# First attention of a two-layer transformer: the order of TensorE's work in a unit written out, and the row maxima split on GpSimd ahead of one transpose

## The chip, the cores and the metric

The kernel runs on one core of a Trainium2 chip. The metric is the device time of one execution in microseconds; before the change it is 1112.01 us, the median of three runs (1110.85 to 1116.76). Engines are named TensorE (PE), VectorE (DVE), ScalarE (ACT), GpSimd (POOL) and SyncE (SP), which issues the DMAs.

## The reference

The kernel computes two layers, each an attention and a mixture of experts. Only the first attention is touched by the change. With B = 2, S = 1024, D = 128, 16 heads of width 8:

```python
xn = _layernorm(x, ln_scale, ln_bias)
q = (xn @ wq).reshape(bs, sl, h, hd).transpose(0, 2, 1, 3)
k = (xn @ wk).reshape(bs, sl, h, hd).transpose(0, 2, 1, 3)
v = (xn @ wv).reshape(bs, sl, h, hd).transpose(0, 2, 1, 3)
scores = jnp.einsum('bhid,bhjd->bhij', q, k)
probs = jax.nn.softmax(scores / jnp.sqrt(jnp.float32(HIDDEN_DIM)), axis=-1)
out = jnp.einsum('bhij,bhjd->bhid', probs, v)
out = out.transpose(0, 2, 1, 3).reshape(bs, sl, -1) + xn
```

The softmax needs each query's maximum over 1024 keys, and it is exact: the maximum is subtracted before the exponential.

## The kernel before, in words

**Tiling.** Two heads make a pair, and 16 pairs (both batches) are worked on one after the other. A unit is one pair with one half of the queries (512), so there are 32 units (`UNITS0`); pair `u // 2`, half `u % 2`. Queries and keys are split in three bfloat16 parts each and stacked on 48 partitions (`q_stack`, `k_stack`), the two heads of a pair at partitions 0 and 64, so that a product of bfloat16 rows gives scores near float32. Two further rows of `q_stack` hold the negative maximum of each query as two bfloat16 parts (high and the rest); `k_stack` has ones there, so a score matmul of 50 rows subtracts the maximum.

**The two passes of a unit.** First the search: eight searches (`search`, L532 for TensorE and L396 for VectorE). Each is two matmuls of 128 queries by 512 keys (both heads) into a bank pair of the ring `max_bank`, and a VectorE maximum over it (L400). After the eighth, VectorE joins the halves (L406) into `maxima`, 128 queries x 8. TensorE transposes this to 8 x 128 (L548, "turn"), VectorE splits it in the bfloat16 parts with two instructions (L413, L415), and SyncE copies them with two DMAs into the two rows of `q_stack` (`subtract`, L275). Then the scores: 16 matmuls of 128 keys by 512 queries (`score`, L580) into three score banks, 16 exponentials on ScalarE (L509) into `probs` (four steps deep), and four value groups (`use`, L593) of four matmuls that add up in one bank. ScalarE copies that bank to `heads` (L481), TensorE turns it (`fold_heads`, L555), and VectorE divides by the sums (L423, L426).

**The ring and the order.** Searches, turns and folds share the ring of two (`RING = 2`). A use of the ring has a number, `PLACE`, the same on TensorE and VectorE, and TensorE may give place i only after VectorE has released place i-2 (`freed`). The order is written out by `ring_of_step`: in unit u at step k (0 to 7) the search number 8u + k + 12 is given (`LEAD = 12`), the turn of unit u+1 follows at step 4 and the fold of unit u-1 at step 6. TensorE's program (end of `layer0`) runs in each step: two scores, the ring's events, and after steps 1, 3, 5, 7 a value group (at step 1 the last one of the unit before). Every engine runs its instructions strictly in this program order. Ahead of unit 0 stand 12 searches and the turn of unit 0 (`ring_before`).

**Waits that matter here.** A score waits for the exponential three scores back (three banks). ScalarE waits before each even step for the value group that frees its `probs` buffer. The first score of a unit waits for the shift DMAs (`shift_in`). The first search of a pair waits for all of the pair's 12 stack loads (`loaded`, L538 with `loads_by`). Each head of a pair takes six loads.

**SyncE's queue.** Its loop over u issues `subtract(u + 1)`, which waits for the turn of unit u+1, and only then `load_head(u // 2 + 2, u % 2)`: the second head of pair p is issued behind the turn of unit 2p-2, which is given in unit 2p-3. In unit 0 the 2 MB load of `rope` follows.

**GpSimd** has, before its copies of values (`stage`), three operations of the residual (L345, L347, L349).

Of the kernel before, what the change touches and what calls it, by code (L numbers as in the profile page):

```python
# [20 lines left out]
P = 128  # L21
# [94 lines left out]
VW = 32  # L116
UNITS0 = B * H0
TILES = TB
LEAD = TILES + 4
FOLD_AT = 6  # L120
RING = 2
SCORES = 3
PROBS = 4
VALUE = HD0 + 1


def ring_of_step(u, k):

    m = TILES * u + k + LEAD
    if m < TILES * UNITS0:  # L130
        yield "search", m
    if k == LEAD - TILES and u + 1 < UNITS0:
        yield "turn", u + 1
    if k == FOLD_AT and u >= 1:
        yield "fold", u - 1


def ring_before():
# [6 lines left out]
def ring_uses():  # L145
    yield from ring_before()
    for u in range(UNITS0):
        for k in range(TB):
            yield from ring_of_step(u, k)
    yield "fold", UNITS0 - 1  # L150


# [3 lines left out]
def layer0(nc, t, d):  # L156
# [3 lines left out]
    with ctx:  # L160
# [6 lines left out]
        def sem(name):  # L167
            return ctx.enter_context(nc.semaphore(name))
# [16 lines left out]
        inverse = sb("inverse", [P, 2, TB])  # L185
        halves = sb("halves", [P, 2, 2, TILES])
        maxima = sb("maxima", [P, 2, TILES])
        shift = sb("shift", [TILES, 2, 2, P], BF16)
        max_bank = [ps(f"max_bank{i}", [P, 2, CH]) for i in range(RING)]
        score_bank = [ps(f"score_bank{i}", [P, CH]) for i in range(SCORES)]  # L190
        summed = ps("summed", [P, CH])
# [14 lines left out]
        loaded = [sem(f"loaded{i}") for i in range(STACKS)]  # L206
        shift_in = [sem(f"shift_in{i}") for i in range(2)]
        staged, padded_set, fold_set = sem("staged"), sem("padded_set"), sem("fold_set")
        filled, freed, joined, high_ready = sem("filled"), sem("freed"), sem("joined"), sem("high_ready")
        score_ready, prob_ready, used = sem("score_ready"), sem("prob_ready"), sem("used")  # L210
        heads_ready, inverse_ready = sem("heads_ready"), sem("inverse_ready")
        NW = 8
# [16 lines left out]
        with nc.Block() as block:  # L229
            @block.sync  # L230
            def _(sp):
# [38 lines left out]
                def subtract(u):  # L270
                    pair, half = divmod(u, 2)
                    sp.wait_ge(freed, PLACE["turn", u] + 1)
                    for part in range(2):
                        row = NST + part
                        sp.dma_start(q_stack[pair % STACKS][row:row + ROW + 1:ROW, half * CH:(half + 1) * CH],  # L275
                                     shift[:, u % 2, part, :]).then_inc(shift_in[u % 2], 16)

                load_x(0)
                sp.dma_start(t.identity[:, :], d["identity"]).then_inc(w_in, 16)
# [32 lines left out]
            @block.gpsimd  # L312
            def _(pool):
                for stack in k_stack:
                    for x in range(2):
                        pool.memset(stack[x * ROW + ROW // 2:(x + 1) * ROW, :], 1.0).then_inc(ones_set, 1)
                pool.wait_ge(ones_set, 2 * STACKS)
                for i in range(2):
                    pool.memset(v_tile[i][:, :, :, :], 0.0).then_inc(padded_set, 1)
                pool.wait_ge(padded_set, 2)  # L320
                for i in range(2):
                    pool.memset(v_tile[i][:, :, :, HD0:HD0 + 1], 1.0).then_inc(padded_set, 1)
                pool.wait_ge(w_in, 16 * NW)
                by_slot = t.identity[:, :].rearrange("p (s w) -> p s w", w=VW)
                pool.tensor_tensor(fold[:, :, :], by_slot[:, 0:2, 0:VALUE], by_slot[:, 2:4, 0:VALUE], ALU.add).then_inc(fold_set, 1)

                for i in range(2 * NCH):
                    which, c, cols = unit(i)
                    pool.wait_ge(mid_ready, i + 1)
                    pool.tensor_tensor(parts[which][:, 2, cols], rest[:, i % 4, :], parts[which][:, 1, cols],  # L330
                                       ALU.subtract).then_inc(lo_ready, 1)

                def stage(pair):
                    if pair >= 2:
                        pool.wait_ge(used, (pair - 1) * 2 * GROUPS)
                    width = 2 * TB * HD0
                    src = t.values0[:, pair * width:(pair + 1) * width].rearrange("p (x t w) -> p x t w", x=2, w=HD0)
                    pool.tensor_copy(v_tile[pair % 2][:, :, :, 0:HD0], src).then_inc(staged, 1)  # L338

                pool.wait_ge(padded_set, 4)  # L340
                pool.wait_ge(v_out, NCH)
                stage(0)
                stage(1)
                scale, bias = (affine[:, i, :].unsqueeze(1).broadcast_to([P, NT, D]) for i in range(2))
                pool.tensor_tensor(normed[:, :, :], normed[:, :, :], scale, ALU.mult).then_inc(residual_step, 1)  # L345
                pool.wait_ge(residual_step, 1)
                pool.tensor_tensor(normed[:, :, :], normed[:, :, :], bias, ALU.add).then_inc(residual_step, 1)  # L347
                pool.wait_ge(residual_step, 2)
                pool.tensor_tensor(t.x[:, :, :], t.x[:, :, :], normed[:, :, :], ALU.add).then_inc(residual_step, 1)  # L349
                for pair in range(2, NPAIR):  # L350
                    stage(pair)

            @block.vector
            def _(dve):
# [41 lines left out]
                def search(m, place):  # L396
# [5 lines left out]
                    if n == TILES - 1:  # L402
                        dve.wait_ge(freed, place + 1)
                        if u >= 2:
                            dve.wait_ge(filled, PLACE["turn", u - 2] + 1)
                        dve.tensor_tensor(maxima[:, u % 2, :], halves[:, u % 2, 0, :], halves[:, u % 2, 1, :], ALU.max).then_inc(joined, 1)  # L406

                def split(u, place):
                    dve.wait_ge(filled, place + 1)
                    if u >= 2:  # L410
                        dve.wait_ge(shift_in[u % 2], 32 * (u // 2))
                    mT = max_bank[place % RING][0:TILES, 0, 0:P]
                    dve.tensor_scalar(shift[:, u % 2, 0, :], mT, -1.0, None, ALU.mult).then_inc(high_ready, 1)  # L413
                    dve.wait_ge(high_ready, u + 1)
                    dve.scalar_tensor_tensor(out=shift[:, u % 2, 1, :], in0=mT, scalar=-1.0, in1=shift[:, u % 2, 0, :],  # L415
                                             op0=ALU.mult, op1=ALU.subtract).then_inc(freed, 1)

                def divide(u, place):
                    pair, half = divmod(u, 2)
# [8 lines left out]
                def take_ring(use):  # L428
                    what, n = use
                    if what == "search":  # L430
                        search(n, PLACE[use])
                    if what == "turn":
                        split(n, PLACE[use])
                    if what == "fold":
                        divide(n, PLACE[use])

# [18 lines left out]
            def _(act):  # L455
# [42 lines left out]
                        mid(i - 1)  # L498
                mid(7)

                for u in range(UNITS0):
                    for k in range(TB):
                        if u * TB + k >= PROBS and k % 2 == 0:
                            done = (u * TB + k - PROBS) // 2 + 1
                            act.wait_ge(used, done)
                        for x in range(2):
                            e = 2 * (u * TB + k) + x
                            act.wait_ge(score_ready, e + 1)
                            act.activation(probs[:, k % PROBS, x, :], score_bank[e % SCORES][:, :], ACT.Exp, scale=SCALE0).then_inc(prob_ready, 1)  # L509
                        if k == 1 and u >= 1:  # L510
                            take(u - 1)
                take(UNITS0 - 1)

            @block.tensor
            def _(pe):
# [28 lines left out]
                    last.then_inc(filled, 1)  # L544

                def turn_maxima(u, place):
                    pe.wait_ge(joined, u + 1)
                    pe.transpose(max_bank[place % RING][0:TILES, 0, 0:P], maxima[:, u % 2, :], t.identity[:, :]).then_inc(filled, 1)  # L548

                def fold_heads(u, place):  # L550
                    pe.wait_ge(heads_ready, u + 1)
# [16 lines left out]
                    if what == "fold":  # L568
                        fold_heads(n, place)

                def score(u, k, x):
                    pair, half = divmod(u, 2)
                    rows, e = slice(x * ROW, x * ROW + NST + 2), 2 * (u * TB + k) + x
                    if k == 0 and x == 0:
                        pe.wait_ge(shift_in[u % 2], 32 * (u // 2 + 1))
                    if u == 0 and k == 0:
                        pe.wait_ge(v_out, NCH)
                    if e >= SCORES:
                        pe.wait_ge(prob_ready, e - SCORES + 1)
# [4 lines left out]
                def use(u, g):  # L584
# [9 lines left out]
                                         start=(g == 0), stop=(g == GROUPS - 1), tile_position=(0, VW * slot))  # L594
                    last.then_inc(used, 1)

                pe.wait_ge(w_in, 16 * NW)
                for c in range(2):
                    turn_in(c)
# [9 lines left out]
                for event in ring_before():  # L609
                    give_ring(event)  # L610
                for u in range(UNITS0):
                    for k in range(TB):
                        for x in range(2):
                            score(u, k, x)
                        for event in ring_of_step(u, k):
                            give_ring(event)
                        if k == 1 and u >= 1:
                            use(u - 1, GROUPS - 1)
                        if k % 2 == 1 and k >= 3:
                            use(u, (k - 3) // 2)  # L620
                use(UNITS0 - 1, GROUPS - 1)
                give_ring(("fold", UNITS0 - 1))

def choose(dve, chain, padded, experts, chosen, top, wanted, marked):

# [1262 lines left out]
```

## Time and profile before

| | |
|---|---|
| median of three runs | 1112.01 us |
| profiled execution | 1116.44 us, span 1114.7 us |
| TensorE busy | 969.4 us (87% of the span) |
| VectorE busy | 728.9 us (65%) |
| ScalarE busy | 629.0 us (56%) |
| GpSimd busy | 331.9 us (30%) |
| searches on VectorE, L400, x256 | 309.9 us, 1224 ns each |
| exponentials, L509, x512 | 267.5 us, 602 ns each |
| value matmuls, L593, x1024 | 138.1 us |

The busy time is an average over all stages. The first attention runs from about 35 to 438 us of the span; the stages behind it are the first mixture, the second attention and the second mixture, whose code is the same in both kernels. A matmul's duration in the profile holds its latency, so that two that follow one another overlap.

### The profile page before, as it was taken

What the parts mean: (1) busy time and instruction counts of PE and PEld (TensorE: products, weight loads), DVE (VectorE), ACT (ScalarE), POOL (GpSimd) and SP (SyncE); (2) the same over time, 40 slices, a digit from 0 to 9 for tenths busy, and PEclk for the clock granted to TensorE, in tenths of its full rate; (3) what the DMA queues carried; (4) which work ended last, traced back from release to release, by engine and by line L of the source; (5) the groups of instructions that cost most, each with busy time, mean ns of one, the idle gap of its engine ahead of it and who ended that gap; (6) DMA issues with size and microseconds to landing.
All of it is one profiled execution on the core that took longest, in us unless ns stands there. A gap on an engine that the chain in (4) does not pass through costs nothing. (4 is left out here: it accounts for less than half of the span.)

```text
span 1114.7 us, 16176 instructions
## 1 busy us (share of the span) xinstructions
PE 969.4 (87%) x5608; PEld 549.5 (49%) x5608; DVE 728.9 (65%) x1443; ACT 629.0 (56%) x1253; POOL 331.9 (30%) x361
## 2 busy tenths in 40 slices
PE   4698888888988985887589999999999999578998
PEld 2222222222222222522467676767677676466997
DVE  6888888888888883424645454545454554565776
ACT  3267777777777775322345546555565554344665
POOL 4600000000000000000665748493756740221222
PEclk9689999999999998689789999999999999797999
DMA  3320000000000001000000000000000000200000
GB/s 66 142 91 15 22 17 15 21 17 15 20 18 16 20 4 24 4 0 14 1 1 10 1 4 4 10 1 6 11 1 1 5 2 1 77 1 1 11 16 15
DMA packets 22745, 20.02 MB, mean 18 GB/s; under 512 B 5064, under 2 KB 17328, under 8 KB 22664
## 3 DMA queue, kind: packets, MB, share of 16 engines
q1 hardware_dynamic: 22664, 18.99, 5.8%
q8 instruction: 45, 0.74, 0.3%
q14 instruction: 36, 0.29, 0.1%
HBM read 14.26 MB, written 4.59 MB: 17 GB/s over the span
## 5 line engine op out<-in xcount | busy, mean ns | idle before, releaser
L400 DVE TENSOR_REDUCE halves<-max_bank 128x2 f32<-128x1024 f32 x256 | 309.9, 1224 | 40.8 <-PE max_bank L542 32.9
L509 ACT ACTIVATE probs<-score_bank 128x512 f32<-128x512 f32 x512 | 267.5, 602 | 108.6 <-PE score_bank L580 108.5
L1390 PE MATMUL a_sum<-a_turned,a_v 128*128 128x512 f32 (+3 forms) x384 | 158.5, 500 | 0.8 <-ACT a_headsT L1319 0.6
L1145 ACT ACTIVATE a_probs<-a_scores,a_lowest 128x896 f32<-128x896 f32 (+7 forms) x128 | 94.9, 741 | 112.4 <-DVE a_lowest L1140 111.9
L580 PE MATMUL score_bank<-q_stack,k_stack 50*128 50x512 bf16 x512 | 133.8, 392 | 27.4 <-ACT probs L509 24.6
L593 PE MATMUL summed<-probs,v_tile 128*32 128x512 f32 x1024 | 138.1, 612 | 0.2 <-ACT probs L509 0.2
L542 PE MATMUL max_bank<-k_stack,q_stack 48*128 48x512 bf16 x512 | 115.2, 393 | 19.4 <-DVE halves L400 19.2
L580 PEld LDWEIGHTS score_bank<-q_stack,k_stack 50*128 50x128 bf16 x512 | 33.7, 93 | 187.0 <-ACT probs L509 141.0
L1140 DVE TENSOR_REDUCE a_lowest<-a_scores 128x1 f32<-128x896 f32 (+7 forms) x128 | 96.2, 755 | 40.6 <-PE a_scores L1134 40.1
L338 POOL COPY v_tile<-values 128x128 f32<-128x128 f32 x16 | 4.7, 296 | 338.8 <-PE summed L593 338.1
L1381 PE MATMUL a_turn<-identity,a_probs 128*128 128x128 f32 x576 | 96.4, 277 | 4.9 <-ACT a_probs L1145 4.9
L1261 DVE COPY a_turned<-a_turn 128x512 f32<-128x512 f32 x96 | 57.4, 598 | 63.2 <-PE a_turn L1381 62.8
L1381 PEld LDWEIGHTS a_turn<-identity,a_probs 128*128 128x128 f32 x576 | 72.2, 143 | 38.3 <-issue 21.0
L1644 DVE SCALAR_TENSOR_TENSOR x<-m_down,m_side,x 128x128 f32<-128x128 f32 x192 | 55.4, 344 | 39.1 <-ACT m_scaled L1735 39.0
L1130 PE MATMUL a_scores<-a_kT,a_qT 128*128 128x512 f32 (+1 forms) x192 | 77.1, 402 | 3.2 <-ACT a_probs L1145 3.2
L1231 POOL TENSOR_TENSOR x<-x,a_part 128x512 f32<-128x512 f32 x32 | 41.0, 1280 | 127.3 <-DVE a_part L1273 127.3
L1797 PEld LDWEIGHTS m_down<-m_w,m_gated 128*128 128x128 f32 x512 | 69.8, 200 | 9.4 <-issue 3.8
L1797 PE MATMUL m_down<-m_w,m_gated 128*128 128x128 f32 x512 | 71.4, 285 | 2.9 <-DVE m_gated L1632 2.4
L1110 ACT ACTIVATE a_swapped<-a_proj 64x512 f32<-64x512 f32 x84 | 49.7, 592 | 40.1 <-DVE a_straight L1101 39.5
L1101 DVE TENSOR_TENSOR a_straight<-a_proj,rope 128x512 f32<-128x512 f32 x43 | 29.7, 692 | 58.8 <-PE a_proj L1085 47.3
L1132 PE MATMUL a_scores<-a_kT,a_qT 128*128 128x512 f32 (+1 forms) x192 | 67.9, 354 | 0.0
L1131 PE MATMUL a_scores<-a_kT,a_qT 128*128 128x512 f32 (+1 forms) x192 | 67.5, 352 | 0.0
(260 smaller groups left out, 1585.9 us busy)
## 6 DMA issues: line engine op xcount, KB each, us to landing
rope<-in_rope SPq DMA_DIRECT2D x1, 2048.0 KB, 8.0
m_w<-in_L_ffn_mlp_w SPq DMA_DIRECT2D x8, 256.0 KB, 4.5
q_parts<-l_q_parts SPq DMA_DIRECT2D x2, 768.0 KB, 4.9
k_parts<-l_k_parts SPq DMA_DIRECT2D x2, 768.0 KB, 6.3
q_stack<-q_parts SPq DMA_DIRECT2D x30, 48.0 KB
k_stack<-k_parts SPq DMA_DIRECT2D x30, 48.0 KB
x<-in_L_attn_x SPq DMA_DIRECT2D x2, 512.0 KB, 4.1
q_stack<-shift SPq DMA_DIRECT2D x64, 2.0 KB
```

The lines of the kernel that those rows point to most:

```text
L400: dve.reduce_max(halves[:, u % 2, half, :].rearrange("p (x t) -> p x t", x=2)[:, :, qt], max_bank[place % RING][:, :, :], AX_X).then_inc(f ...
L509: act.activation(probs[:, k % PROBS, x, :], score_bank[e % SCORES][:, :], ACT.Exp, scale=SCALE0).then_inc(prob_ready, 1)
L542: last = pe.matmul(max_bank[place % RING][:, x, :], q_stack[stack][rows, queries], k_stack[stack][rows, half * CH:(half + 1) * CH], start= ...
L580: pe.matmul(score_bank[e % SCORES][:, :], k_stack[pair % STACKS][rows, k * P:(k + 1) * P], q_stack[pair % STACKS][rows, half * CH:(half + ...
L593: last = pe.matmul(summed[VW * slot:VW * (slot + 1), :], v_tile[pair % 2][:, x, k, :], probs[:, k % PROBS, x, :], start=(g == 0), stop=(g ...
L1130: pe.matmul(dst, qT[0][:, b, q, rows], kT[0][:, b, first:first + cols], start=True, stop=False)
L1132: pe.matmul(dst, qT[1][:, b, q, rows], kT[0][:, b, first:first + cols], start=False, stop=first + cols < width)
L1140: dve.tensor_reduce(out=lowest[:, n % 8:n % 8 + 1], in_=scores[n % 2][:, 0:row_width(n)], op=ALU.max, axis=AX_X, negate=True).then_inc(low ...
L1145: act.activation(probs[:, k % 2, c, 0:row_width(n)], scores[n % 2][:, 0:row_width(n)], ACT.Exp, bias=lowest[:, n % 8:n % 8 + 1], accum_out ...
L1381: last_turn = pe.transpose(turn_bank[m % 2][:, c * P:(c + 1) * P], probs[:, k % 2, c, j * P:(j + 1) * P], t.identity[:, :])
L1390: pe.matmul(sum_bank[:, skipped(k, j):CH], v[:, BLOCKS[k][0], j, :], turned[:, m % SLOTS, skipped(k, j):CH], start=(j == 0), stop=(TURNED_ ...
L1797: last = pe.matmul(down_bank[n % DOWN][:, k, :], left, right, start=True, stop=True)
```

## The change

TensorE's order in a unit is written out by hand (`unit_of`) in place of the regular step. `LEAD` becomes 15, so that the first ring place of unit u is the last search of unit u+1, and the first search of unit u+2 is the second place. The ring of a unit is now search x5, turn, search, fold, search, search.

The split in bfloat16 parts moves ahead of the transpose. GpSimd makes from `maxima` (128 x 8) the bfloat16 rounding `high16`, its float32 copy, and the difference, the last two side by side in `shift_parts` (128 x 16). One transpose turns both, and one VectorE copy writes both to `shift` (16 x 128, bfloat16). The sign moves to `k_stack`, whose extra rows hold -1. The DMAs of `subtract` have the same sizes and stand at the same place in SyncE's loop.

```diff
-LEAD = TILES + 4
-FOLD_AT = 6
+LEAD = 2 * TILES - 1
+RING_OF_UNIT = ("search",) * 5 + ("turn", "search", "fold", "search", "search")
+
+def ring_of_unit(u):
+    m = TILES * u + LEAD
+    for what in RING_OF_UNIT:
+        if what == "search":
+            yield ("search", m) if m < TILES * UNITS0 else None
+            m += 1
+        if what == "turn":
+            yield ("turn", u + 1) if u + 1 < UNITS0 else None
+        if what == "fold":
+            yield ("fold", u - 1) if u >= 1 else None
...
-                        pool.memset(stack[x * ROW + ROW // 2:(x + 1) * ROW, :], 1.0).then_inc(ones_set, 1)
+                        pool.memset(stack[x * ROW + ROW // 2:(x + 1) * ROW, :], -1.0).then_inc(ones_set, 1)
...
+                def split_maxima(u):
+                    pool.wait_ge(joined, u + 1)
+                    if u >= 1:
+                        pool.wait_ge(split, 3 * u)
+                    pool.tensor_copy(high16[:, u % 2, :], maxima[:, u % 2, :]).then_inc(split, 1)
+                    if u >= 2:
+                        pool.wait_ge(filled, PLACE["turn", u - 2] + 1)
+                    pool.wait_ge(split, 3 * u + 1)
+                    pool.tensor_copy(shift_parts[:, u % 2, 0, :], high16[:, u % 2, :]).then_inc(split, 1)
+                    pool.wait_ge(split, 3 * u + 2)
+                    pool.tensor_tensor(shift_parts[:, u % 2, 1, :], maxima[:, u % 2, :], high16[:, u % 2, :], ALU.subtract).then_inc(split, 1)
...
-                for pair in range(2, NPAIR):
-                    stage(pair)
+                for u in range(UNITS0):
+                    split_maxima(u)
+                    if u % 2 == 1 and u // 2 + 1 in range(2, NPAIR):
+                        stage(u // 2 + 1)
...
-                def split(u, place):
+                def take_shift(u, place):
                     dve.wait_ge(filled, place + 1)
                     if u >= 2:
                         dve.wait_ge(shift_in[u % 2], 32 * (u // 2))
-                    mT = max_bank[place % RING][0:TILES, 0, 0:P]
-                    dve.tensor_scalar(shift[:, u % 2, 0, :], mT, -1.0, None, ALU.mult).then_inc(high_ready, 1)
-                    dve.wait_ge(high_ready, u + 1)
-                    dve.scalar_tensor_tensor(out=shift[:, u % 2, 1, :], in0=mT, scalar=-1.0, in1=shift[:, u % 2, 0, :],
-                                             op0=ALU.mult, op1=ALU.subtract).then_inc(freed, 1)
+                    dve.tensor_copy(shift[:, u % 2, :], max_bank[place % RING][0:2 * TILES, 0, 0:P]).then_inc(freed, 1)
...
-                    pe.wait_ge(joined, u + 1)
-                    pe.transpose(max_bank[place % RING][0:TILES, 0, 0:P], maxima[:, u % 2, :], t.identity[:, :]).then_inc(filled, 1)
+                    pe.wait_ge(split, 3 * u + 3)
+                    pe.transpose(max_bank[place % RING][0:2 * TILES, 0, 0:P], shift_parts[:, u % 2, :, :].rearrange("p a n -> p (a n)"), t.identity[:, :]).then_inc(filled, 1)
...
+                def unit_of(u):
...
+                    next_scores(1)
+                    next_place()
+                    next_scores(2)
+                    next_place()
+                    next_scores(1)
+                    if u >= 1:
+                        use(u - 1, GROUPS - 1)
+                    next_scores(1)
+                    next_place()
+                    next_scores(1)
+                    next_place()
+                    next_scores(2)
+                    use(u, 0)
+                    next_place()
+                    next_scores(3)
+                    next_place()
+                    use(u, 1)
+                    next_place()
+                    next_scores(2)
+                    next_place()
+                    next_scores(1)
+                    next_place()
+                    next_scores(2)
+                    next_place()
+                    use(u, 2)
...
-                    for k in range(TB):
-                        for x in range(2):
-                            score(u, k, x)
-                        for event in ring_of_step(u, k):
-                            give_ring(event)
-                        if k == 1 and u >= 1:
-                            use(u - 1, GROUPS - 1)
-                        if k % 2 == 1 and k >= 3:
-                            use(u, (k - 3) // 2)
+                    unit_of(u)
```

`next_scores(n)` issues the unit's next n score matmuls, and `next_place()` the next event of the ring. ScalarE's loop is written over one counter with the same order of instructions.

## Rows read from the trace of the kernel before

**Rows 1.** Windows: length, busy us of PE, PEld, DVE, ACT, POOL, clock, DMA share, GB/s

```profile
66.00:413.00 347.00, 310.57 (x2121) 87.61 (x2117) 309.28 (x378) 256.70 (x493) 4.15 (x14) 1.00 0.07 23
```

**Rows 2.** Timeline of VectorE, one unit: start us, busy us, instruction [idle before it <-releaser]

```profile
251.53 0.17 DVE L406 TENSOR_TENSOR maxima<-halves 128x8 f32<-128x8 f32 x1
251.81 1.23 DVE L400 TENSOR_REDUCE halves<-max_bank 128x2 f32<-128x1024 f32 x1
252.95 0.27 DVE L413 TENSOR_SCALAR shift<-max_bank 8x128 bf16<-8x128 f32 x1
253.25 0.28 DVE L415 SCALAR_TENSOR_TENSOR shift<-max_bank,shift 8x128 bf16<-8x128 f32 x1
253.52 1.23 DVE L400 TENSOR_REDUCE halves<-max_bank 128x2 f32<-128x1024 f32 x1
255.06 1.23 DVE L400 TENSOR_REDUCE halves<-max_bank 128x2 f32<-128x1024 f32 x1 [0.31 <-PE max_bank L542]
256.20 0.20 DVE L423 RECIPROCAL inverse<-max_bank 128x8 f32<-128x8 f32 x1
256.43 0.22 DVE L426 TENSOR_TENSOR attn<-max_bank,inverse 128x64 f32<-128x64 f32 x1
...
263.50 0.17 DVE L406 TENSOR_TENSOR maxima<-halves 128x8 f32<-128x8 f32 x1
```

**Rows 3.** Timeline of TensorE's matmuls in the same unit

```profile
251.16 0.39 PE L580 MATMUL score_bank<-q_stack,k_stack 50*128 50x512 bf16 x2
251.38 0.38 PE L542 MATMUL max_bank<-k_stack,q_stack 48*128 48x512 bf16 x2
...
253.09 0.39 PE L542 MATMUL max_bank<-k_stack,q_stack 48*128 48x512 bf16 x2 [0.41 <-DVE halves L400]
253.41 1.06 PE L593 MATMUL summed<-probs,v_tile 128*32 128x512 f32 x8
254.41 0.39 PE L580 MATMUL score_bank<-q_stack,k_stack 50*128 50x512 bf16 x2
...
254.95 1.07 PE L555 MATMUL max_bank<-fold,heads 128*128 128x18 f32 x8
```

**Rows 4.** Timeline of ScalarE in the same unit

```profile
258.14 2.06 ACT L509 ACTIVATE probs<-score_bank 128x512 f32<-128x512 f32 x4 [0.69 <-PE score_bank L580]
```

**Rows 5.** Timeline of SyncE's queue, one unit: first and last of seven merged rows

```profile
253.56 1.12 SPq L275 DMA_DIRECT2D q_stack<-shift  x2
...
258.05 0.29 SPq L268 DMA_DIRECT2D k_stack<-k_parts  x1
```

**Rows 6.** Windows, behind the last load of that unit

```profile
260.00:260.20 0.20, 0.20 (x4) 0.00 (x0) 0.20 (x1) 0.20 (x1) 0.00 (x0) 1.00 0.00 0
```

**Rows 7.** DMA issues of the page: KB each, median us from issue to landing

```profile
first_q<-l_q_parts SPq DMA_DIRECT2D x1, 32.0 KB, 2.5
```

**Rows 8.** Windows around low clocks: first attention's start, second attention

```profile
56.00:60.00 4.00, 4.00 (x18) 0.59 (x15) 2.86 (x4) 1.89 (x4) 0.00 (x0) 0.50 0.00 0
...
64.00:68.00 4.00, 3.69 (x26) 0.76 (x27) 3.65 (x4) 3.26 (x8) 0.00 (x0) 0.91 0.42 81
...
553.00:556.00 3.00, 0.47 (x5) 0.29 (x3) 1.79 (x3) 2.73 (x4) 2.78 (x4) 1.00 0.00 0
556.00:559.60 3.60, 2.93 (x8) 2.33 (x9) 0.15 (x1) 1.50 (x4) 3.37 (x3) 0.53 0.00 0
```

**Rows 9.** Timeline of TensorE in the second attention

```profile
556.67 0.79 PE L1130 MATMUL a_scores<-a_kT,a_qT 128*128 128x512 f32 x1 [3.20 <-ACT a_probs L1145]
```

**Rows 10.** Timeline of all engines, 30 to 84 us, start of the first attention

```profile
45.04 0.64 DVE L406 TENSOR_TENSOR maxima<-halves 128x8 f32<-128x8 f32 x1
...
45.74 4.50 POOL L349 TENSOR_TENSOR x<-x,l_normed 128x2048 f32<-128x2048 f32 x1
...
52.20 0.61 PE L580 MATMUL score_bank<-q_stack,k_stack 50*128 50x512 bf16 x2 [2.78 <-DMA q_stack<-shift]
...
56.41 1.93 PE L593 MATMUL summed<-probs,v_tile 128*32 128x512 f32 x8
```

More of the change, by code:

```diff
@@ L124 @@
 VALUE = HD0 + 1
[L127 to L135, printed above, removed]
+RING_OF_UNIT = ("search",) * 5 + ("turn", "search", "fold", "search", "search")
[9 more added lines that the diff above has]
+            yield ("fold", u - 1) if u >= 1 else None
 def ring_before():
@@ L147, in ring_uses @@
     for u in range(UNITS0):
-        for k in range(TB):
-            yield from ring_of_step(u, k)
+        yield from filter(None, ring_of_unit(u))
     yield "fold", UNITS0 - 1
@@ L187, in layer0 @@
         maxima = sb("maxima", [P, 2, TILES])
-        shift = sb("shift", [TILES, 2, 2, P], BF16)
+        shift_parts = sb("shift_parts", [P, 2, 2, TILES])
+        shift = sb("shift", [2 * TILES, 2, P], BF16)
+        high16 = sb("high16", [P, 2, TILES], BF16)
         max_bank = [ps(f"max_bank{i}", [P, 2, CH]) for i in range(RING)]
@@ L208, in layer0 @@
         staged, padded_set, fold_set = sem("staged"), sem("padded_set"), sem("fold_set")
-        filled, freed, joined, high_ready = sem("filled"), sem("freed"), sem("joined"), sem("high_ready")
+        filled, freed, joined, split = sem("filled"), sem("freed"), sem("joined"), sem("split")
         score_ready, prob_ready, used = sem("score_ready"), sem("prob_ready"), sem("used")
@@ L275, in subtract @@
                         sp.dma_start(q_stack[pair % STACKS][row:row + ROW + 1:ROW, half * CH:(half + 1) * CH],
-                                     shift[:, u % 2, part, :]).then_inc(shift_in[u % 2], 16)
+                                     shift[part * TILES:(part + 1) * TILES, u % 2, :]).then_inc(shift_in[u % 2], 16)
                 load_x(0)
@@ L404, in search @@
                         if u >= 2:
-                            dve.wait_ge(filled, PLACE["turn", u - 2] + 1)
+                            dve.wait_ge(split, 3 * (u - 1))
                         dve.tensor_tensor(maxima[:, u % 2, :], halves[:, u % 2, 0, :], halves[:, u % 2, 1, :], ALU.max).then_inc(joined, 1)
-                def split(u, place):
+                def take_shift(u, place):
                     dve.wait_ge(filled, place + 1)
@@ L432, in take_ring @@
                     if what == "turn":
-                        split(n, PLACE[use])
+                        take_shift(n, PLACE[use])
                     if what == "fold":
@@ L499, in _ @@
                 mid(7)
[L501 to L505, printed above, removed]
-                        for x in range(2):
-                            e = 2 * (u * TB + k) + x
-                            act.wait_ge(score_ready, e + 1)
-                            act.activation(probs[:, k % PROBS, x, :], score_bank[e % SCORES][:, :], ACT.Exp, scale=SCALE0).then_inc(prob_ready, 1)
-                        if k == 1 and u >= 1:
-                            take(u - 1)
+                for step in range(UNITS0 * TB):
+                    u, k = divmod(step, TB)
+                    if step >= PROBS and step % 2 == 0:
+                        done = (step - PROBS) // 2 + 1
+                        act.wait_ge(used, done)
+                    for x in range(2):
+                        e = 2 * step + x
+                        act.wait_ge(score_ready, e + 1)
+                        act.activation(probs[:, step % PROBS, x, :], score_bank[e % SCORES][:, :], ACT.Exp, scale=SCALE0).then_inc(prob_ready, 1)
+                    if k == 1 and u >= 1:
+                        take(u - 1)
                 take(UNITS0 - 1)
@@ L569, in give_ring, with score @@
                         fold_heads(n, place)
-                def score(u, k, x):
+                def score(e):
+                    step, x = divmod(e, 2)
+                    u, k = divmod(step, TB)
                     pair, half = divmod(u, 2)
-                    rows, e = slice(x * ROW, x * ROW + NST + 2), 2 * (u * TB + k) + x
+                    rows = slice(x * ROW, x * ROW + NST + 2)
                     if k == 0 and x == 0:
                         pe.wait_ge(shift_in[u % 2], 32 * (u // 2 + 1))
-                    if u == 0 and k == 0:
+                    if e == 0:
                         pe.wait_ge(v_out, NCH)
@@ L595, in use, with next_scores, next_place @@
                     last.then_inc(used, 1)
+                def unit_of(u):
+                    scores = iter(range(2 * TB * u, 2 * TB * (u + 1)))
+                    ring = ring_of_unit(u)
+                    def next_scores(count):
+                        for _ in range(count):
+                            score(next(scores))
+                    def next_place():
+                        event = next(ring)
+                        if event is not None:
+                            give_ring(event)
+                    next_scores(1)
[23 more added lines that the diff above has]
+                    use(u, 2)
                 pe.wait_ge(w_in, 16 * NW)
@@ L611, in _ @@
                 for u in range(UNITS0):
-                    for k in range(TB):
-                        for x in range(2):
-                            score(u, k, x)
-                        for event in ring_of_step(u, k):
-                            give_ring(event)
-                        if k == 1 and u >= 1:
-                            use(u - 1, GROUPS - 1)
-                        if k % 2 == 1 and k >= 3:
-                            use(u, (k - 3) // 2)
+                    unit_of(u)
                 use(UNITS0 - 1, GROUPS - 1)
```

## The prediction, made before the changed kernel was run

> **What bounds the kernel now.** I read the windows of all engines first, since only the first attention changes. From 66 to 413 us VectorE is busy for 309.3 of 347 us and TensorE for 310.6, ScalarE for 256.7; the granted clock is 1.00 and the DMA share 0.07 [rows 1]. Nothing is full, so the order in time decides. VectorE's timeline [rows 2] repeats: the maxima's join starts at 251.53 and again at 263.50, so a unit takes 11.97 us. In it a search follows a search after 1.14 us; the join makes 0.28 and delays the search before it (0.41 over eight plain searches); the two split instructions 0.57 (252.95 to 253.52); reciprocal and divide 0.45. That is 8 x 1.14 + 0.41 + 0.57 + 0.45 = 10.55 us; the other 1.42 is waiting, mostly on TensorE's searches (0.31 at 255.06). TensorE's timeline [rows 3] gives its steps: a value group holds it for 1.00 (253.41 to 254.41), a pair of scores or one score 0.22 (251.16 to 251.38), a search pair 0.22 (the same row distance), a fold 1.07. VectorE's search of 251.81 ended at 253.04, TensorE's next search started at 253.09 and was read at 253.52: a search is read at the earliest 1.23 + 0.05 + 0.43 = 1.71 us after the start of the one two ring places ahead. ScalarE needs about 0.49 an exponential (four in 2.06) [rows 4], 8.4 with the heads' copy in a unit: not the bound.
>
> **The new order, walked.** E0 to E9 are the ring places of a unit; E0 starts on VectorE at 0, and the places are given out in the order search x5, turn, search, fold, search, search.
> VectorE reads E0 at 0, E1 at 1.55 (join), E2 at 2.69, E3 at 3.83, E4 at 4.97, the turn E5 at 6.11. TensorE is ahead until there: E2 is given at 1.79 behind a value group, E4 at 4.27 behind the next. The turn can be given when E3 is released (5.11) and then the value group runs to 6.38; E6, whose bank E4 released at 6.25, is given at 6.38 and read at 6.81. The turn's copy ended at 6.40, so 0.41 of waiting is left. E7 (fold) starts at 7.95, E8 at 8.52 (0.12 of waiting for the bank), E9 at 9.66, the next E0 at 10.80. Check by the sum: 9.12 + 0.41 + 0.29 + 0.45 + 0.53 of waits = 10.80. Against 11.97 the unit is 1.17 us shorter: 0.28 is the second split instruction, 0.89 is order. The depth of two ring places gives part of the faster turn back, as the 0.41 shows.
>
> **Costs I can't read off.** The new VectorE copy (16x128 out of a bank) isn't in the trace: between 0.17 (the 128x8 join) and 0.28 (the old second instruction); I take 0.27, the first one's, since it too reads a bank with few rows. GpSimd's three instructions on 128x8 lie between E0's join (1.5) and the turn (5.1). Between nothing and 0.64 each, the longest that a 128x8 operation took here [rows 10], they fit: at most 1.9 of 3.6 us. The transposed block has 16 columns in place of 8: between 0 and 0.27 more on TensorE, I take 0, since a pass streams the same 128 columns; at that place TensorE waits anyway. The join took 0.64 at 45.04 while GpSimd ran an operation from 128x2048, and 0.17 at 251.53 with GpSimd idle [rows 2, 10]. The Trainium skill (SBUF — State Buffer, Who interferes with whom) says that a VectorE instruction with two SBUF inputs is locked out by a GpSimd instruction that reads SBUF, and a reduction is not. By that rule the new GpSimd work costs nothing, as it runs during reductions out of banks; without it the price would be 0.47 more on a join, 14 us over 30 units.
>
> **A deadline that moves.** The lead grows from 12 to 15 searches, so the first search of unit u+2 goes from step 4 of unit u to E1 of unit u. For even u it waits for all twelve loads of its pair. SyncE issues the last six behind the two shift DMAs of the turn in the unit before; this order isn't touched. The shift DMAs start at 253.56, 0.03 after VectorE's second instruction, and the last load is issued at 258.05 [rows 5]. By 260.0 the DMA engines are idle (share 0.00) [rows 6]. A 32 KB transfer took 2.5 us from issue to landing [rows 7], so I put the landing at 260.55, 7.0 us after the shifts' issue (bounds 6.4, when the data is through, and 7.5). Before, that load had a whole unit of 11.97 us. Now: turn copied at 6.40, landing at 6.43 + 7.00 = 13.43, which is 2.63 of the next unit, and TensorE is at E1 at 0.14. It stands idle from -0.22, when its last two scores end, to 2.68.
> The stalled unit, by the same steps: E1 is read at 3.11. TensorE then has a score, a value group and another score in front of E2: 4.77. E3 is read at 5.91. Score 8 waits for the exponential of score 5, which waits for the heads' copy behind that value group; the value group follows at 5.67, E4 is read at 7.10 in place of 4.97, and the rest keeps this 2.1 us. A pair of units takes 21.6 + 2.1 = 23.7 us where it took 23.95. This happens in the 14 even units from 2 to 28 (pairs 2 to 15; pair 1 is loaded long before). So 14 x 0.25 = 3.5 us come back, and 1.2 from the one unit left over between unit 1 and unit 30. The scores' own wait for the shifts costs nothing: they are issued at 6.43 and 7.0, land by 9.5 at 2.5 each, and the next unit's first score is at 9.75; that cover is 0.25 us thin.
>
> **The clock.** TensorE idles 2.9 us in each such stall; its waits in the old unit are of the size of the 0.41 before 253.09 [rows 3]. Where it idled 3.20 us before 556.67 [rows 9], the granted clock was 1.00 in 553 to 556 and 0.53 in 556 to 559.6 [rows 8]. At the start of the attention the clock was 0.50 in 56 to 60, with TensorE busy throughout, and 0.91 only in 64 to 68 [rows 8]. At half clock a value group took 1.93 in place of 1.06 [rows 3, 10]. The stalled unit has no slack for that: walked again with the low clock for 3.5 us after the stall, E4 comes 1.4 us later than above, for 5 us 1.8, for 7 us 2.6. I take 5 us (between the 3.6 of the window after 556 and the 12 at the start, nearer to the first, since value groups follow at once) and that it falls in 85 of 100 stalls: 1.5 us each, 21 us over 14. The Trainium skill (TensorE: Matmul & The Clock Gate, Loop structure matters more than you think) speaks against this change: it names a DMA wait between matmuls as what makes the engine go cold. The trace agrees, with the 0.53.
>
> **The start.** The first turn now needs GpSimd's split, and GpSimd is in its residual operations until 45.74 + 4.50 = 50.24 [rows 10]; before, the first join at 45.04 went straight to TensorE. With three small operations the turn is copied at about 51.9; the searches 9 to 14 follow, and the first score comes behind the fifteenth, when its bank is given (51.9 + 4 x 1.14, about 57), where it was at 52.20 on a late DMA [rows 10]. That is +4.8. The end has three searches less in unit 30, which gives 0.4 to 1.3 back. I take +4, bounds 0 and 8.
>
> **Sum.** 1116.4 (profiled execution; span 1114.7) - 3.5 - 1.2 + 21 + 4 = 1136.7. The median of the three runs, 1112.0, lies 4.4 below that execution: 1132 us, 1.8% slower. A difference under 0.5% (5.6 us) counts as no change.
>
> **Rivals.**
> 1. The stall comes, but the clock holds (the idle time falls so that it doesn't count): 1116.4 - 4.7 + 4, less 4.4: 1111, no change; with the landing at its bounds, 0.6 earlier or 0.5 later, 8 less or 7 more. For it: in 553 to 556 the clock was still 1.00 while the engine already idled [rows 8]. Against: it fell right behind, and the 2.9 us here are nearly the 3.20 there. Chance 0.20.
> 2. The loads don't bind, because they land early or the turn comes early: 29 units x 1.17 = 34 less, +4 for the start: 1082, faster by 2.7%. For it: six of the twelve loads land a unit earlier, and the last six are small. Against: one semaphore counts all twelve, and 4.5 us between the turn and E1 stand against 7.0. It holds only if turn to landing is under 4.6 us. Chance 0.15.
> 3. The low clock lasts for the rest of the unit, as it did from 52 to 64 with a busy TensorE: about 5 us more on each pair than at full clock, 14 x 5 = 70: 1181. Chance 0.10.
> 4. Something not seen, either side: 0.05.
> The forecast has 0.50, with its own range 1120 to 1150. The range 1095 to 1165 leaves out most of rival 2 and of rival 3, 2 in 10. Faster: rival 2 and the lower third of rival 1, 0.21; no change 0.14; slower 0.65.
>
> **What would show it.** Right: in the waits, TensorE's search waiting for the DMA of the stack loads, some 14 times, 2 to 3 us each; a granted clock below 1.00 in the windows from 90 to 400 us; even and odd units of unequal length (about 14.4 and 10.8 us between joins). The order alone is right if odd units take 10.8; the split on GpSimd is harmless if no turn waits for it after the first. I am wrong on the deadline if no search waits for a DMA, and on the clock if it stays at 1.00 despite such waits.

## The result, and the profile after

The changed kernel takes 1134.7 us (median of 4 runs, 1129.5 to 1142.4), 1.9% longer than the kernel before, whose median over four runs is now 1114.3: ratio 1.0191, 95% interval 1.0124 to 1.0259. The profiled execution took 1129.5 us, the shortest of the four, with a span of 1127.7 us against 1114.7. So every length below is read from an execution that lies 5.2 us under the median. The waits between 90 and 400 us (columns: engine line <- releaser: us in total, times, longest):

```profile
ACT probs L524 <- PE score_bank L597: 71.6, 113, 3.1
DVE halves L419 <- PE max_bank L557: 51.1, 53, 2.3
...
PE max_bank L557 <- DMA k_stack<-k_parts: 33.4, 12, 3.2
```

The last line did not exist before: TensorE's search waits for a pair's loads, 12 times in this stretch, 2.8 us each. One such place in the timeline, with SyncE's queue ahead of it:

```profile
200.15 1.12 SPq L280 DMA_DIRECT2D q_stack<-shift  x2
...
204.65 0.29 SPq L273 DMA_DIRECT2D k_stack<-k_parts  x1
205.91 0.17 DVE L425 TENSOR_TENSOR maxima<-halves 128x8 f32<-128x8 f32 x1
...
207.68 0.39 PE L557 MATMUL max_bank<-k_stack,q_stack 48*128 48x512 bf16 x2 [3.14 <-DMA k_stack<-k_parts]
207.91 0.38 PE L597 MATMUL score_bank<-q_stack,k_stack 50*128 50x512 bf16 x1
208.11 1.23 DVE L419 TENSOR_REDUCE halves<-max_bank 128x2 f32<-128x1024 f32 x1 [2.02 <-PE max_bank L557]
208.22 1.07 PE L610 MATMUL summed<-probs,v_tile 128*32 128x512 f32 x8
...
210.28 2.36 DVE L419 TENSOR_REDUCE halves<-max_bank 128x2 f32<-128x1024 f32 x2 [0.95 <-PE max_bank L557]
210.47 0.70 PE L597 MATMUL score_bank<-q_stack,k_stack 50*128 50x512 bf16 x2
211.09 1.82 PE L610 MATMUL summed<-probs,v_tile 128*32 128x512 f32 x8
```

SyncE's rows are to be compared with [rows 5]: the last load is issued 4.50 us behind the shifts and the search runs 7.53 us behind them. Over the 14 such searches this is 6.88 to 7.61 us, 7.19 on average. A value group took 1.07 at 208.22 and 1.82 at 211.09. The windows show why (the last three columns are the granted clock, the DMA share and GB/s):

```profile
205.00:206.80 1.80, 0.00 (x0) 0.00 (x0) 1.05 (x2) 0.78 (x2) 0.44 (x3) 1.00 0.16 41
206.80:207.60 0.80, 0.00 (x0) 0.00 (x0) 0.00 (x0) 0.00 (x0) 0.14 (x1) 1.00 0.03 10
207.60:209.00 1.40, 1.32 (x11) 0.30 (x11) 0.89 (x1) 0.60 (x1) 0.00 (x0) 1.00 0.00 0
...
209.00:212.70 3.70, 3.70 (x20) 0.73 (x16) 2.69 (x3) 2.73 (x5) 0.29 (x1) 0.54 0.00 0
```

From 205 to 207.6 no matmul runs while the loads come in, and in the window from 209.0, 1.3 us after the search, the clock is at its lower level (0.54). The start, against [rows 10]:

```profile
43.63 0.64 DVE L425 TENSOR_TENSOR maxima<-halves 128x8 f32<-128x8 f32 x1
...
44.33 4.49 POOL L366 TENSOR_TENSOR x<-x,l_normed 128x2048 f32<-128x2048 f32 x1
48.76 0.19 POOL L349 CAST high<-maxima 128x8 bf16<-128x8 f32 x1
...
49.64 0.37 PE L563 MATMUL max_bank<-identity,shift_parts 128*16 128x128 f32 x1 [6.51 <-POOL shift_parts L355]
...
50.05 0.28 DVE L431 CAST shift<-max_bank 16x128 bf16<-16x128 f32 x1 [4.64 <-PE max_bank L563]
...
55.67 0.63 PE L597 MATMUL score_bank<-q_stack,k_stack 50*128 50x512 bf16 x1
```

The first join ends at 44.27, and the turn comes at 49.64, since GpSimd is in its residual until 48.8 and splits only then. The length of a unit, read from join to join on VectorE, sums up the rest. Before, all are 11.97 or 11.98 but the first two. After, the 14 units whose second ring place waits for loads ("even") and the ones behind them ("odd"), in us:

```
even: 15.62 14.87 13.37 13.09 13.42 14.60 13.95 15.94 13.93 14.27 13.12 12.99 15.21 14.15   mean 14.18
odd:  10.67 or 10.68, every one
```

### The profile page after: what moved, and what is told of

The parts are those of the page before. It is cut to its first block and busy times, and to the rows that moved or that the text cites. A ratio compares the mean times of both kernels' runs of the same rounds, so it can differ in the third digit from the quotient of the medians.

```text
span 1127.7 us, 16301 instructions
## 1 busy us (share of the span) xinstructions
PE 966.4 (86%) x5608; PEld 551.6 (49%) x5608; DVE 712.0 (63%) x1411; ACT 632.1 (56%) x1253; POOL 350.4 (31%) x457
## 5 line engine op out<-in xcount | busy, mean ns | idle before, releaser
L419 DVE TENSOR_REDUCE halves<-max_bank 128x2 f32<-128x1024 f32 x256 | 300.7, 1221 | 66.1 <-PE max_bank L557 64.0
L557 PE MATMUL max_bank<-k_stack,q_stack 48*128 48x512 bf16 x512 | 120.9, 415 | 55.7 <-DMA k_stack<-k_parts 39.2
L610 PE MATMUL summed<-probs,v_tile 128*32 128x512 f32 x1024 | 147.2, 649 | 0.5 <-ACT probs L524 0.5
L597 PE MATMUL score_bank<-q_stack,k_stack 50*128 50x512 bf16 x512 | 140.2, 402 | 3.6 <-ACT probs L524 3.4
L349 POOL CAST high<-maxima 128x8 bf16<-128x8 f32 x32 | 6.1, 191 | 315.0 <-DVE maxima L425 315.0
L557 PEld LDWEIGHTS max_bank<-k_stack,q_stack 48*128 48x128 bf16 x512 | 26.3, 96 | 154.1 <-DVE halves L419 69.6
L597 PEld LDWEIGHTS score_bank<-q_stack,k_stack 50*128 50x128 bf16 x512 | 37.3, 96 | 89.6 <-ACT probs L524 42.3
```

The source lines that it names most:

```text
L419: dve.reduce_max(halves[:, u % 2, half, :].rearrange("p (x t) -> p x t", x=2)[:, :, qt], max_bank[place % RING][:, :, :], AX_X).then_inc(f ...
L557: last = pe.matmul(max_bank[place % RING][:, x, :], q_stack[stack][rows, queries], k_stack[stack][rows, half * CH:(half + 1) * CH], start= ...
L597: pe.matmul(score_bank[e % SCORES][:, :], k_stack[pair % STACKS][rows, k * P:(k + 1) * P], q_stack[pair % STACKS][rows, half * CH:(half + ...
L610: last = pe.matmul(summed[VW * slot:VW * (slot + 1), :], v_tile[pair % 2][:, x, k, :], probs[:, k % PROBS, x, :], start=(g == 0), stop=(g ...
```

## The experiments

**All loads ahead of the shifts.**

```diff
                 for u in range(UNITS0):
-                    if u + 1 < UNITS0:
-                        subtract(u + 1)
                     pair, x = u // 2 + 2, u % 2
...
                         load_head(pair, x)
+                    if u + 1 < UNITS0:
+                        subtract(u + 1)
```

> The changed kernel, but SyncE issues the six stack loads of a step ahead of the two shift DMAs of that step, not behind them. Theory (a deadline of the loads, and the clock that falls in the wait): no search waits for a DMA, all units are as long as the odd ones are now (10.67 us between joins in place of 14.1 in the even ones), the clock stays 1.00 from 90 to 400 us. 14 x 3.4 = 48 us less than the changed kernel: about 1087, 2.4% faster than before. Rival (the even units are long for another reason, such as GpSimd's copy of values or the heads' copy): even units stay near 14 us, the time near 1135. Rival (the shifts are now late behind the loads' issue): the first score of each unit waits, all units are 1 to 3 us longer.

Measured: 1078.2 us, ratio 0.9725 (0.9688 to 0.9761). Every unit from the fourth join on takes 10.67 or 10.68, no search waits for a DMA, and the clock holds:

```profile
90.00:400.00 310.00, 290.97 (x2098) 87.42 (x2094) 274.07 (x333) 257.63 (x495) 19.19 (x97) 1.00 0.06 17
```

The place of the loads in SyncE's queue turned a gain of 2.7% (3.0% by the medians, 1078.2 against 1111.2) into a loss of 1.9%. The time is 9 us under the 1087 that I expected. Of the 53.6 us between the spans 1127.7 and 1074.1, 49 lie in the attention (14 x 3.51) and 4 in the stages behind it, whose code is the same and whose time differs from execution to execution (669 to 678 us in the ten profiles). The expectation also started from the median of the changed kernel and took the price of a stall from its shortest execution.

**The wait filled with work**, in `search`, ahead of the wait for the loads (`FILL = 10`; their results are overwritten):

```diff
                     if n == 0 and side == 0:
+                        if pair >= 2:
+                            for _ in range(FILL):
+                                for x in range(2):
+                                    rows = slice(x * ROW, x * ROW + NST)
+                                    pe.matmul(max_bank[place % RING][:, x, :], q_stack[(pair - 1) % STACKS][rows, 0:P],
+                                              k_stack[(pair - 1) % STACKS][rows, 0:CH], start=True, stop=True, tile_position=(x * ROW, 0))
                         pe.wait_ge(loaded[stack], loads_by(pair))
```

> The changed kernel, with ten pairs of extra search matmuls (their results are overwritten by the search behind them) ahead of the wait for a pair's loads, so that TensorE works for 2.2 us of the 2.9 in which it idled. The stall stays, the clock should hold. Theory (the clock is a part of its own): even units 12.8 to 13.0 us, all alike, in place of 13.0 to 15.9; clock 1.00 from 90 to 400 us; 14 x 1.2 = 17 us less than the changed kernel, about 1118. Rival (the low clock costs nothing, only the wait does): the even units and the time stay as they are, 1135. Rival (the extra work delays the search itself): even units longer than 14.

Measured: 1115.0 us, ratio 1.0041 (1.0022 to 1.0060). Even units 12.83 to 13.86, mean 13.25; odd ones 10.67. Clock 1.00 in all windows, where the changed kernel has 0.91 from 200 to 300:

```profile
200.00:300.00 100.00, 94.66 (x703) 29.57 (x699) 84.98 (x101) 74.37 (x142) 6.42 (x31) 1.00 0.06 19
```

So of the 3.51 us that an even unit loses, 2.58 (13.25 - 10.67) are the wait and 0.93 (14.18 - 13.25) the clock. The filler did not move the search itself: VectorE reads it 7.66 us behind the shifts on average, against 7.70 in the changed kernel. The changed kernel's own five even units without a low clock near them (12.99, 13.09, 13.12, 13.37, 13.42) say the same, 13.20 on average. The nine others average 14.73, so one fall of the clock costs about 1.5 us. That the even units would be all alike, 12.8 to 13.0, was wrong: the landing of the loads differs from unit to unit. The search is read 7.24 to 8.27 us behind the shifts, and the units of 12.83 to 13.86 follow it. More work on TensorE made the kernel faster than the changed one.

**One load ahead, then two.** `load_head` issues its first `AHEAD` DMAs ahead of `subtract(u + 1)` and the rest behind it.

```diff
+                        load_head(pair, x, range(AHEAD))
                     if u + 1 < UNITS0:
                         subtract(u + 1)
+                    if pair < NPAIR:
+                        load_head(pair, x, range(AHEAD, 6))
```

> The changed kernel, with the first of the six loads issued ahead of the shifts and five behind: the last load is issued 0.75 us earlier. Theory: the search is read 0.75 us earlier, TensorE idles 2.1 us in place of 2.9, the clock falls in fewer stalls; even units 12.0 to 13.0 us on most, so 14 x 1.3 = 18 us less, about 1117. If the wait is not set by the last load's landing, nothing changes (1135).

> The changed kernel, with two of the six loads ahead of the shifts and four behind: the last load is issued 1.5 us earlier than in the changed kernel. Theory: TensorE still waits about 1.0 to 1.5 us for the loads, VectorE 0.3 to 1; the clock falls seldom or never; even units 11.0 to 12.3 us, about 1095 (between 1078 of all ahead and 1121 of one ahead). Rival (a step: any wait brings the low clock and the same loss as with one ahead): about 1118.

Measured: 1120.6 us (ratio 1.0100, 1.0071 to 1.0128) and 1094.5 us (0.9847, 0.9815 to 0.9879). The wait shrinks with the issue time of what is still behind the shifts; first the waits with one ahead, then with two:

```profile
PE max_bank L562 <- DMA k_stack<-k_parts: 26.5, 13, 2.4
```

```profile
PE max_bank L562 <- DMA k_stack<-k_parts: 13.4, 13, 1.5
```

2.0 and 1.0 us each, against 2.8. The profile with one ahead is of the shortest of its four executions (1113.3 us, the others 1120.2 to 1124.1). Even units: mean 13.51 with one ahead, 11.27 to 11.57 with two but for one of 13.00. With one ahead I had expected the clock to fall less often; the profile shows it at its lower level in eleven stretches between 83 and 401 us, against nine of the changed kernel (83 to 411 us), and the units without such a stretch near them take 12.04 to 12.23. With two ahead the clock fell once, in the unit of 13.00, behind an idle stretch of 1.5 us; the other thirteen stretches are of 0.9 to 1.2 us.

**The same order of issue in the kernel before.** The diff of the first experiment, on the kernel before.

> The kernel before, with only the loads issued ahead of the shifts. Theory: there the loads have a whole unit of slack, so it stays at 1112 to 1116, units at 11.97 us. Rival (loads ahead are good in themselves, by less DMA traffic beside the shifts): faster by more than 5 us.

Measured: 1111.7 us, ratio 1.0005 (0.9989 to 1.0020), units 11.98. The loads had slack there; only the longer lead made their place matter.

**The split back on VectorE, in the new order with loads ahead.** `take_shift` becomes the old `split`, `turn_maxima` the old one, `split_maxima` goes, the ones are +1.

```diff
-                    dve.tensor_copy(shift[:, u % 2, :], max_bank[place % RING][0:2 * TILES, 0, 0:P]).then_inc(freed, 1)
+                    mT = max_bank[place % RING][0:TILES, 0, 0:P]
+                    dve.tensor_scalar(shift[:, u % 2, 0, :], mT, -1.0, None, ALU.mult).then_inc(high_ready, 1)
+                    dve.wait_ge(high_ready, u + 1)
+                    dve.scalar_tensor_tensor(out=shift[:, u % 2, 1, :], in0=mT, scalar=-1.0, in1=shift[:, u % 2, 0, :],
+                                             op0=ALU.mult, op1=ALU.subtract).then_inc(freed, 1)
```

> The kernel of e1 (new order, loads ahead of the shifts), but the maxima are turned first and split by two VectorE instructions, as before the change; the ones are +1 again, GpSimd does no split. Theory (behind the turn VectorE waits for the next search anyway, 0.53 us in e1, since only two ring places exist): the second instruction of 0.28 us fits in that wait, the unit stays at 10.67 to 10.70 us and the split on GpSimd is worth nothing in a unit; at the start the first turn no longer waits for GpSimd, which gives 3 to 5 us: about 1074. Rival (each VectorE instruction taken away shortens the unit): 10.95 us a unit, 29 x 0.28 = 8 us more, less the start: about 1083.

Measured: 1073.8 us, ratio 0.9659 (0.9641 to 0.9678), units still 10.67. With the next experiment it is the fastest version; the two can't be told apart. TensorE and VectorE around the turn with the split on GpSimd (loads ahead), then with VectorE's own two instructions:

```profile
256.61 1.07 PE L610 MATMUL summed<-probs,v_tile 128*32 128x512 f32 x8
257.24 0.27 DVE L431 CAST shift<-max_bank 16x128 bf16<-16x128 f32 x1
...
257.61 0.39 PE L557 MATMUL max_bank<-k_stack,q_stack 48*128 48x512 bf16 x2
...
258.04 1.23 DVE L419 TENSOR_REDUCE halves<-max_bank 128x2 f32<-128x1024 f32 x1 [0.53 <-PE max_bank L557]
```

```profile
252.34 1.06 PE L612 MATMUL summed<-probs,v_tile 128*32 128x512 f32 x8
252.98 0.27 DVE L430 TENSOR_SCALAR shift<-max_bank 8x128 bf16<-8x128 f32 x1
253.28 0.28 DVE L432 SCALAR_TENSOR_TENSOR shift<-max_bank,shift 8x128 bf16<-8x128 f32 x1
253.33 0.39 PE L559 MATMUL max_bank<-k_stack,q_stack 48*128 48x512 bf16 x2
...
253.77 1.23 DVE L417 TENSOR_REDUCE halves<-max_bank 128x2 f32<-128x1024 f32 x1 [0.21 <-PE max_bank L559]
```

VectorE's search starts 0.80 and 0.79 us after its first instruction on the turn: what the split saves is given back as waiting for TensorE's next search. TensorE gives that search 1.00 and 0.99 us after the start of the value group that stands between it and the turn, in both kernels. With two instructions it gives it (253.33) before the second one has ended (253.56), so it doesn't wait for the split.

**The first split ahead of the residual's last two operations**, on the kernel with loads ahead.

```diff
                 pool.wait_ge(residual_step, 1)
+                split_maxima(0)
                 pool.tensor_tensor(normed[:, :, :], normed[:, :, :], bias, ALU.add).then_inc(residual_step, 1)
...
                 for u in range(UNITS0):
-                    split_maxima(u)
+                    if u >= 1:
+                        split_maxima(u)
```

> The kernel of e1, but GpSimd splits the maxima of unit 0 behind the first of its three residual operations, not behind the third. Theory: the first turn is given at about 44.7 us of the span in place of 49.6, the first score comes at about 52, bound by the landing of its shifts in a busy DMA queue, in place of 55.7: 3 to 4 us less than e1, about 1075, and 3.3% under the kernel before. Rival (the clock is low there and TensorE is the bound of unit 0): no change against e1, 1078.

Measured: 1074.3 us, ratio 0.9654 (0.9632 to 0.9676), units 10.67. The turn is no longer held, and the first score now waits for its shifts:

```profile
45.33 0.37 PE L565 MATMUL max_bank<-identity,shift_parts 128*16 128x128 f32 x1 [1.68 <-POOL shift_parts L355]
...
52.28 0.60 PE L599 MATMUL score_bank<-q_stack,k_stack 50*128 50x512 bf16 x1 [0.70 <-DMA q_stack<-shift]
```

From the first search to the last divide the profile has 367.4 us with loads ahead, and 362.1 both here and with the split on VectorE. So the start was worth 5.3 us in the attention, and with it repaired the split on either engine gives the same time. The medians differ by 4 (1078.2 to 1074.3) and were taken on two chips; the two profiled executions took the same time (1075.9 and 1075.8), since the stages ahead of the attention and behind it took as much more in the second.

**The split on GpSimd in the old order.** `LEAD`, `ring_of_step` and TensorE's loop as before the change, the rest as changed.

> The changed kernel with the order and the lead of the kernel before (turn one search behind the join), so only the split has moved to GpSimd. Theory: the turn waits for three GpSimd instructions of 0.19 us and their hops, 0.9 us in all, in front of two scores and a search on TensorE; the 0.3 us that VectorE saves don't make up for it: units of 12.2 to 12.8 us in place of 11.97, 7 to 25 us slower than before, about 1127. Rival (the split alone is a gain, since the old order had 1.4 us of waits anyway): units at or under 11.97, time at or under 1111.

Measured: 1118.1 us, ratio 1.0025 (1.0001 to 1.0048). The ten times form two groups, four of 1109.6 to 1112.0 and six of 1118.0 to 1118.6; the profile is of the second, and why there are two stays open. So the median says little here, and the unit's length counts. Units take 12.00, below the 12.2 I had as a lower end: TensorE stands idle for 0.93 us ahead of the turn, but a unit is only 0.03 longer than before. That VectorE's shorter copy makes up for the rest is likely, not shown.

```profile
253.77 0.27 PE L560 MATMUL max_bank<-identity,shift_parts 128*16 128x128 f32 x1 [0.93 <-POOL shift_parts L352]
...
254.08 0.28 DVE L428 CAST shift<-max_bank 16x128 bf16<-16x128 f32 x1
```

## Why the prediction was right, step by step

- **The order.** Predicted 10.80 us for a unit without a stall, measured 10.67. The prediction put 0.89 of the gain down to the order and 0.28 to the second split instruction; with the split back on VectorE the unit is still 10.67, so the 0.28 was not there, and all of the gain is order.
- **The deadline.** The even units are the ones that stall, from 2 to 28. Predicted 2.1 us of loss without the clock, measured 2.58. Two terms were too small. The prediction had the search read 1.56 us late (3.11 in place of 1.55); in the five stalled units at full clock it is read 1.56 to 1.98 late, 1.76 on average, in part since the loads land later than the 7.0 us assumed (7.19 on average, 7.53 in the unit shown). And the walk behind the stall turned the 1.56 into 2.13, 0.57 more; in these five units the loss is 0.76 or 0.77 more than the lateness. A pair at full clock takes 23.92 (13.25 + 10.67) against 23.7 predicted and 23.95 before: order and deadline cancel, a little more closely than the forecast had it.
- **The clock.** Predicted 1.5 us a stall (1.8 for a fall, in 85 of 100 stalls), measured 0.93 in this profile: 1.5 for a fall, in nine stalls of 14. The row that the prediction used, 0.53, stood behind a wait for ScalarE; the 0.54 after 209.0 stands behind a wait for a DMA.
- **The start.** From the first search on VectorE to the first score 16.33 us before (35.87 to 52.20), 21.21 after (34.46 to 55.67): +4.9, predicted 4.8.
- **The sum.** From the first search to the last divide 401.8 us before, 416.6 after: +14.8, which is 14 x (2.58 + 0.93) = 49.1, less 29 x 1.30 = 37.8, plus 4.9, with -1.4 for unit 0 and the end. The prediction had +20.3; the clock term was 8 too large for this execution (21 against 13), and the even and odd units' own errors (0.48 more, 0.13 less) partly cancel.
- **The closeness is partly luck.** The forecast had 1136.7 for the profiled execution, and it took 1129.5. It had 1132 for the median, by taking off the 4.4 that the profiled execution before lay above its median, and here the profiled execution lies 5.2 below. The three other executions had a lower granted clock (0.909 to 0.921 against 0.926) and spans of 1132.6 to 1140.6, which fits more or longer falls of the clock in them; they have no profile that could show it. By the ratios 1.0191 and 1.0041 the filler gave back 1.5%, about 17 us with an uncertainty of several, so the clock term of a typical execution probably lies between the 13 of this one and the predicted 21.
- **GpSimd's work beside VectorE** cost nothing that shows: its three instructions take 0.19 to 0.20 us, and the join keeps its 0.17 us in the steady part.

That the waits for the loads and the clock are separate causes is shown by the filler; that both come from SyncE's order is shown by the first experiment. Why the clock falls in one stall and not in the next of the same length stays open.

## What to carry to other kernels

When work is moved ahead, list every wait that the moved instruction carries and ask of each releaser when it is issued now; here a longer lead ate the slack of loads that stood in a queue behind something unrelated. Put what waits for nothing ahead of what waits in a DMA queue. An instruction taken off an engine gains only if what follows is ready earlier: here VectorE's next search had to wait for TensorE, which had a value group in front of it, however short the copy was.

## What was not expected of the hardware

The clock fell behind idle stretches of TensorE of 1.6 to 2.4 us in at least as many cases (eleven stretches on 14 waits) as behind those of 2.5 to 3.2 us (nine on 14), once behind 1.5 us, and never behind the other thirteen of that run, of 0.9 to 1.2 us. Length alone doesn't decide: stalls of 2.95 and 3.00 us left the clock up, and one of 2.49 was followed by a fall. With repeated work on old operands in the wait, it stayed at the higher level through all 14 stalls.
